# Second attention: maxima turned in 32x32 blocks and moved by DMAs instead of through TensorE

## What is computed

```python
# x (2, 1024, 128), 16 heads of 64
xn = rms_norm(x, gamma)
q, k, v = split(xn @ w_qkv)              # per head: 1024 x 64
sim = einsum('bhid,bhjd->bhij', q * 64 ** -0.5, k)
attn = softmax(sim, axis=-1)             # over the 1024 keys
out = einsum('bhij,bhjd->bhid', attn, v) @ w_out
```

## Time and profile before

| what | us |
|---|---|
| median of 3 runs | 1117.93 |
| lowest and highest run | 1117.87 and 1118.39 |
| span of the profiled execution, first to last instruction | 1115.6 |
| around that span, up to the median of the runs | 2.3 |
| granted TensorE clock, mean | 1.000 |

### The profile page before, as it was taken

One profiled execution on the slowest core, in us unless ns is written; L12 is line 12 of the kernel. 1 busy time (PEld: TensorE's weight loads), 2 busy tenths in 40 slices (PEclk: granted clock), 3 DMA queues, 4 the chain that ended last, 5 costly groups with the idle time before them and its releaser, 6 DMA issues.

```text
span 1115.6 us, 21181 instructions
## 1 busy us (share of the span) xinstructions
PE 1100.7 (99%) x8399; PEld 706.2 (63%) x8399; DVE 846.0 (76%) x1246; ACT 591.8 (53%) x939; POOL 795.7 (71%) x524
## 2 busy tenths in 40 slices
PE   9999999999999999999999999999999999999998
PEld 7899889777755555455455455455455555457886
DVE  4868897666686878878878888888888888896554
ACT  4534334566666555555555455555555555554443
POOL 5778888754367889888888888898889898950000
PEclk9999999999999999999999999999999999999999
DMA  7322223300000002000000000000000000000000
GB/s 251 127 77 80 95 77 115 94 24 1 1 1 1 1 1 105 1 1 1 1 1 1 1 1 1 1 1 1 1 1 1 1 1 1 1 1 10 9 1 19
DMA packets 25601, 30.97 MB, mean 28 GB/s; under 512 B 2064, under 2 KB 21904, under 8 KB 24224
## 3 DMA queue, kind: packets, MB, share of 16 engines
q1 hardware_dynamic: 25184, 29.62, 7.9%
q10 hardware_dynamic: 320, 0.01, 0.0%
HBM read 20.19 MB, written 9.44 MB: 27 GB/s over the span
## 4 chain that ended last, share of the span: by engine, by line
PE 88%; DVE 7%; issue 2%; ACT 2%; POOL 2%; DVEq 0%; POOLq 0%; ACTq 0%
PE o_ps L1713 19%; PE mx_ps L1667 7%; PE st_ps L1697 5%; PE st_ps L1691 5%; PE st_ps L1694 5%; PE ha_banks L647 5%; PE bank L2126 3%; PE bank L2127 3%; PE bank L2128 3%; PE mx_ps L1600 3%; PE pj_ps L1619 2%; PE pj_ps L1611 2%; PE ha_banks L698 2%; PE ha_banks L667 2%; PE ha_banks L709 2%
## 5 line engine op out<-in xcount | busy, mean ns | idle before, releaser
L2040 POOL TENSOR_TENSOR acc<-acc,prob 128x1024 f32<-128x1024 f32 x192 | 468.6, 2440 | 61.9 <-ACT prob L1861 51.7
L1861 ACT ACTIVATE prob<-st_ps 128x1024 f32<-128x1024 f32 x256 | 248.5, 1023 | 206.4 <-PE st_ps L1697 206.3
L1713 PE MATMUL o_ps<-prob,v_cur 128*64 128x512 f32 x1024 | 245.7, 599 | 0.0
L1932 DVE TENSOR_REDUCE mx_part<-mx_ps 128x1 f32<-128x512 f32 x258 | 164.9, 667 | 72.0 <-PE mx_ps L1667 72.0
L1713 PEld LDWEIGHTS o_ps<-prob,v_cur 128*64 128x64 f32 x1024 | 68.1, 136 | 96.2 <-issue 77.5
L1935 DVE TENSOR_REDUCE mx_part<-mx_ps 128x2 f32<-128x1024 f32 x78 | 93.7, 1201 | 44.1 <-PE mx_ps L1667 44.1
L1951 DVE RECIPROCAL rden<-rden 128x128 f32<-128x128 f32 x128 | 120.6, 942 | 0.0
L1667 PEld LDWEIGHTS mx_ps<-k_hi,q_hi 64*128 64x128 f32 x414 | 46.6, 183 | 107.0 <-issue 94.6
L1667 PE MATMUL mx_ps<-k_hi,q_hi 64*128 64x512 f32 x414 | 111.7, 457 | 1.5 <-DVE mx_part L1935 0.8
L1697 PE MATMUL st_ps<-q_hi,d_lo 64*128 64x512 f32 x512 | 100.8, 390 | 0.0
L2040 POOL TENSOR_TENSOR acc<-prob 128x1024 f32<-128x1024 f32 x32 | 76.1, 2378 | 26.2 <-PE pj_ps L1596 18.9
(11 more groups left out here) (419 smaller groups left out, 2349.3 us busy)
## 6 DMA issues: line engine op xcount, KB each, us to landing
v_rows<-ha_v SPq DMA_DIRECT2D x8, 1024.0 KB, 3.9
ha_vt<-v_rows SPq DMA_DIRECT2D x16, 512.0 KB, 4.0
h_w<-in_h SPq DMA_DIRECT2D x2, 1024.0 KB, 8.1
w_raw<-in_w SPq DMA_DIRECT2D x8, 192.0 KB, 3.2
head_wkv<-in_wkv SPq DMA_DIRECT2D x2, 512.0 KB, 6.0
m_w<-in_m SPq DMA_DIRECT2D x3, 256.0 KB, 3.1
out<-fin SPq DMA_DIRECT2D x3, 256.0 KB, 2.3
sel_raw<-in_sel SPq DMA_DIRECT2D x1, 576.0 KB, 11.5
```

The source lines that it names most:

```text
L1713: mm = pe.matmul(o_ps[rows(h), :], v_cur[:, m % 2, j, rows(h)], prob[:, (16 * m + slot) % RING, h, :], start=(j == 0), stop=(j == KT - 1), ...
L1861: act.activation(prob[:, n % RING, :, :], st_ps[:, slot % 2, :, :], ACT.Exp, scale=SCALE).then_inc(s_exp, 1)
L1932: dve.reduce_max(mx_part[:, h, i, keys:keys + 1], maxima_banks(q, n)[h], AX_X).then_inc(s_mxr, 1)
L2040: pool.tensor_tensor(total, old, new, ALU.add).then_inc(s_acc, 1)
```

## The change

The unit `("tr", half)` goes. `mx_row` becomes 128 x 32, of which eight columns are written. VectorE turns it in blocks of 32x32 into `mx_turned` right behind L1939, after waiting for its own result and for the DMAs that read the block before. SP gets a function `sync_max`, called for each half of each step: it waits for the turned block, and issues four DMAs, one for each block of 32 partitions. Each takes eight rows of 32 numbers and writes them into one row a head of `q_max` (partitions 0 and 64), all else in `q_max` stays zero from a fill at the start. The product with minus ones moves to the end of the slots 0, 1, 8 and 9, and waits for the DMAs in slots 0 and 8 alone. The pattern `diag` and its two DMAs go, and the load of the last network's weights is issued behind the DMAs of step 3.

```diff
-    mx_row = early.sb("mx_row", [P, 2, HD])
+    mx_row, mx_turned = early.sb("mx_row", [P, BLOCK], F32R), early.sb("mx_turned", [P, BLOCK])
...
-    BEFORE = (QK[0], QK[1], QK[2], ("tr", 1), QK[3], ("v", 0), ("v", 1), ("tr", 0))
+    BEFORE = (QK[0], QK[1], QK[2], None, QK[3], ("v", 0), ("v", 1), None)
...
-        sp.wait_ge(s_fill, 1)
-        sp.dma_start(diag[0:KT, :], a["diag"]).then_inc(s_wo, 16)
-        sp.dma_start(diag[HD:HD + KT, :], a["diag"]).then_inc(s_wo, 16)
...
+    def sync_max(sp, q, half):
+        sp.wait_ge(s_turned, 2 * q + half + 1)
+        if q:
+            sp.wait_ge(s_st, 16 * (q - 1) + KT * half + 2)
+        else:
+            sp.wait_ge(s_fill, 1)
+        heads = q_max[0:P:HD, half_of(half)].bitcast(F32).rearrange("h (i n) -> h i n", i=TT)
+        for block in range(TT):
+            of = slice(block * BLOCK, block * BLOCK + BLOCK)
+            sp.dma_start(heads[:, :, of], mx_turned[of.start:of.start + 2 * TT, :]).then_inc(s_max, 16)
...
-        elif u[0] == "tr":
-            pe.wait_ge(s_row, 2 * q + u[1] + 1)
-            for h in range(2):
-                mm = pe.matmul(to[rows(h), 0:P], mx_row[:, h, :], c.ident[:, :], start=True, stop=True,
-                               skip_group_check=True)
...
-        if fresh:
-            for h in range(2):
-                pe.matmul(st[:, h, :], minus[rows(h), :], q_max[rows(h), half_of(half)], start=True, stop=True)
...
+        if fresh:
+            if j == 0:
+                pe.wait_ge(s_max, 16 * TT * (2 * m + half + 1))
+            for h in range(2):
+                mm = pe.matmul(st[:, h, :], minus[rows(h), :], q_max[rows(h), half_of(half)], start=False, stop=True,
+                               skip_group_check=True)
...
-    def vector_spread_max(dve, q, u):
-
-        half = u[1]
-        dve.wait_ge(s_pj, count_of[q, u])
-        dve.tensor_tensor(q_max[:, half_of(half)].rearrange("p (i n) -> p i n", i=TT),
-                          unit_bank(q, u)[:, 0:P].unsqueeze(1).to_broadcast([P, TT, P]),
-                          diag[:, half_of(half)].rearrange("p (i n) -> p i n", i=TT), ALU.mult).then_inc(s_max, 1)
...
-            dve.reduce_max(mx_row[:, :, first:first + TT], mx_part[:, :, first:first + TT, :], AX_X)\
+            dve.reduce_max(mx_row[:, 0:2 * TT].rearrange("p (h i) -> p h i", h=2), mx_part[:, :, first:first + TT, :], AX_X)\
                .then_inc(s_row, 1)
+            turned = 2 * q + n // 8
+            dve.wait_ge(s_row, turned + 1)
+            if turned:
+
+                dve.wait_ge(s_max, 16 * TT * turned)
+            dve.transpose(mx_turned[:, :], mx_row[:, :].bitcast(F32)).then_inc(s_turned, 1)
...
-        if at_b and at_b[1][0] == "tr":
-            vector_spread_max(dve, *at_b)
...
-        pool.memset(diag[:, :], 0.0).then_inc(s_fill, 1)
+        pool.memset(q_max[:, :].bitcast(F32), 0.0).then_inc(s_fill, 1)
...
-                end.sync_raw(sp)
+                for m in range(STEPS):
+                    for half in range(HALVES):
+                        t2.sync_max(sp, m, half)
+                    if m == LOADED:
+                        end.sync_raw(sp)
```

More of the change, by code:

```diff
@@ L1366, in second_attention @@
     s = Const()
+    BLOCK = P // TT
     w_raw = early.sb("w_raw", [P, PAIRS, W_V])
     wo = early.sb("wo", [P, PAIRS, P])
-    diag = early.sb("diag_all", [P, LEN])
     q_max = early.sb("q_max", [P, LEN], F32R)
@@ L1401, in second_attention @@
     s_st, s_exp, s_acc, s_pv = (at.sem(n) for n in ("s_st", "s_exp", "s_acc", "s_pv"))
-    s_mx, s_mxr, s_row, s_max = (at.sem(n) for n in ("s_mx", "s_mxr", "s_row", "s_max"))
+    s_mx, s_mxr, s_row, s_turned, s_max = (at.sem(n) for n in ("s_mx", "s_mxr", "s_row", "s_turned1", "s_max"))
     s_v, s_den, s_osum, s_rcp, s_on, s_out = (
@@ L1422, in second_attention @@
     SLOT_CUT = 12
-    BEFORE = (QK[0], QK[1], QK[2], ("tr", 1), QK[3], ("v", 0), ("v", 1), ("tr", 0))
+    BEFORE = (QK[0], QK[1], QK[2], None, QK[3], ("v", 0), ("v", 1), None)
     AFTER = {1: ("den", 1), 3: ("out", 0), 5: ("den", 0), 7: ("out", 1)}
-    AHEAD = {**{u: 1 for u in QK}, ("v", 0): 1, ("v", 1): 1, ("tr", 0): 1, ("tr", 1): 0, ("den", 0): 0,
+    AHEAD = {**{u: 1 for u in QK}, ("v", 0): 1, ("v", 1): 1, ("den", 0): 0,
              ("den", 1): -1, ("out", 0): -1, ("out", 1): -1}
@@ L1440, in before @@
     def before(m, b):
+        if BEFORE[b] is None:
+            return None
         q = m + AHEAD[BEFORE[b]]
@@ L1503, in aside @@
         return three(q - AHEAD[u], b)
-    turns = [(0, QK[3]), (0, ("v", 0)), (0, ("v", 1)), (0, QK[2]), (0, ("tr", 0))]
+    turns = [(0, QK[3]), (0, ("v", 0)), (0, ("v", 1)), (0, QK[2])]
     turns += [u for m in range(STEPS + 1) for b in range(BATCHES)
@@ L1553, in unit_out @@
                 pe.wait_ge(s_d if t else s_lo, 2 * q + half + 1)
-        elif u[0] == "tr":
-            pe.wait_ge(s_max, 2 * q + u[1] + 1)
         elif u[0] == "v":
@@ L1578, in tensor_unit @@
             pe.wait_ge(e.s_su, e.ALL - 1)
-        elif (q, u) == (0, ("tr", 0)):
-            pe.wait_ge(s_row, 1)
         elif aside(q, u):
@@ L1615, in tensor_unit @@
             if q == 0 and half == 0:
-                pe.wait_ge(s_wo, 16 * (2 + PAIRS))
+                pe.wait_ge(s_wo, 16 * PAIRS)
             pe.wait_ge(s_on, 2 * q + half + 1)
@@ L1672, in tensor_scores @@
         half, j = slot // KT, slot % KT
-        if j == 0:
-            pe.wait_ge(s_max, 2 * m + half + 1)
         if m == 0 and slot == 0:
@@ L1685, in tensor_scores @@
         fresh = j < 2
-        if fresh:
-            for h in range(2):
-                pe.matmul(st[:, h, :], minus[rows(h), :], q_max[rows(h), half_of(half)], start=True, stop=True)
         upper = kh[:, tile(j)] if fresh else dh[:, tile(j - 2)]
         for h in range(2):
-            pe.matmul(st[:, h, :], upper[rows(h), :], qh[rows(h), half_of(half)], start=False, stop=False,
+            pe.matmul(st[:, h, :], upper[rows(h), :], qh[rows(h), half_of(half)], start=fresh, stop=False,
                       skip_group_check=True)
@@ L1696, in tensor_scores @@
         for h in range(2):
-            mm = pe.matmul(st[:, h, :], dl[rows(h), tile(j)], qh[rows(h), half_of(half)], start=False, stop=True,
+            mm = pe.matmul(st[:, h, :], dl[rows(h), tile(j)], qh[rows(h), half_of(half)], start=False, stop=not fresh,
                            skip_group_check=True)
+        if fresh:
[4 more added lines that the diff above has]
+                               skip_group_check=True)
         mm.then_inc(s_st, 1)
@@ L1744, in tensor_begin @@
         tensor_maxima(pe, 0, 8)
-        tensor_unit(pe, 0, ("tr", 0))
         tensor_maxima(pe, 0, 9)
@@ L1785, in unit_bank @@
             return st_ps[:, 0, QK.index(u), :]
-        if (q, u) == (0, ("tr", 0)):
-            return st_ps[:, 0, 0, :]
         return mx_ps[:, 1, :] if aside(q, u) else pj_ps[:, :]
@@ L1883, in vector_start @@
         dve.wait_ge(head.s_yc, head.TURNS)
-        dve.memset(mx_row[:, :, :], 0.0).then_inc(s_rowfill, 1)
+        dve.memset(mx_row[:, :].bitcast(F32), 0.0).then_inc(s_rowfill, 1)
         dve.memset(mx_part[:, :, :, :], 0.0).then_inc(s_rowfill, 1)
@@ L1967, in vector_begin @@
             vector_maxima(dve, 0, n)
-        dve.wait_ge(s_wo, 16 * (2 + PAIRS))
-        vector_spread_max(dve, 0, ("tr", 0))
         vector_maxima(dve, 0, 9)
@@ L2044, in second_attention @@
     s.tensor_begin, s.scalar_begin, s.vector_begin = tensor_begin, scalar_begin, vector_begin
+    s.sync_max = sync_max
     s.vector_start, s.gpsimd_start, s.gpsimd_begin = vector_start, gpsimd_start, gpsimd_begin
@@ L2396, in two_layers @@
         STARTED = 4
+        LOADED = 3
         SPLIT = 8
```

## The result

The changed kernel takes 1125.2 us (median of 4 runs, 1123.59 to 1125.79), the kernel before in the same session 1118.16 (1117.87 to 1118.42): the ratio is 1.0062, 95% interval 1.0047 to 1.0076. It is slower, by 7.0 us; the forecast was 1124.7. The profiled execution took 1125.26 with a span of 1123.0, so the 2.3 us around the span are unchanged, and the span grew by 7.4.

What follows compares the result with a forecast made beforehand. TensorE's and VectorE's chains reach the projection L1619 at the same moment, so TensorE wins nothing unless VectorE gets shorter. Terms +7.6 and -0.8 sum to +6.8 us: 1115.6 + 2.3 + 6.8 = 1124.7, range 1116 to 1136.

Steps and rivals of the forecast that it cites:

- What bounds it: At the projection L1619, TensorE's and VectorE's chains arrive together; TensorE wins nothing unless VectorE gets shorter.
- Step 1: Removed transposing matmuls on TensorE: 10.6 us in 28 steady batches, all falling into the projection's wait, put at 0.
- Step 2: Removed 32 products with the diagonal, 0.68 each, behind the last reduction: worth 0, only lengthening idle time.
- Step 3: Added VectorE transposition and wait before the reciprocal: 0.27 a batch, 28 times, 7.6 us (5.6 to 14.6).
- Step 4: Product with minus one moved from first to last in its slots, as many matmuls of the same shape: cost 0.
- Step 5: Four added SP DMAs per half: landed B+5.2 to B+5.7, needed at B+6.2 (B: batch start), cost 0.
- Step 6: Four other units: two in step 0 gain 0.8 us; one in step 15, 0; the start, 0 (-0.6 to +0.7).
- TensorE gets its time back: Rival: the bank does not hold the projection's load, batches end 0.38 earlier: -11.8 us, 1106.1; chance 0.13.
- The DMAs are late: Rival: slower issues land the DMAs 0.4 to 0.9 late on 28 halves, 11 to 25 us more: 1136 to 1150; chance 0.13.
- VectorE's addition hides: Rival: transposition slips under its neighbours and own wait is free: -0.8 to +2.0 us, about 1118.5; chance 0.10.

Runs made afterwards that it cites:

- experiment 2: Changed kernel with two unread matmuls of the removed shape put back in each of the 28 batches: 1123.71 us, ratio 1.0051.
- experiment 1: Kernel before, plus VectorE's wait for the row of maxima and a transposition into a tile nobody reads: 1124.69 us, ratio 1.0055.
- Experiment 3: Kernel before, with the reciprocal of the 28 batches moved behind the second reductions: 1118.01 us, ratio 0.9999.
- experiment 5: Changed kernel with eight unread matmuls ahead of TensorE's first wait for the DMAs: 1123.88 us, ratio 1.0048.
- experiment 4: Changed kernel with the reciprocal of the 28 batches moved behind the second reductions: 1109.80 us, ratio 0.9922.
- experiment 8: Changed kernel with eight DMAs of one head each for a half instead of four: 1206.88 us, ratio 1.0789.
- experiment 9: Kernel before, plus a VectorE transposition of a constant tile, without the wait for the row: 1119.96 us, ratio 1.0013.
- experiment 10: Changed kernel with the reciprocal moved, three unread matmuls before the first DMA wait, and ScalarE issuing two of the first four DMAs: 1107.86 us, ratio 0.9904.

## Why the prediction was right, and where it was not

The mechanism is the one forecast and its experiments hold it: the removed matmuls are worth nothing in the 28 batches (experiment 2), VectorE's addition sets the growth (experiment 1), and the number, 1124.7 for 1125.2, is nearer than its terms deserve; that nearness is luck. Term by term:

- *What bounds it.* Right, and closer than the text could know: both chains reach the projection at one moment. Experiment 3 shows TensorE's own chain alone at 2.27 after the row's reduction; VectorE's alone is worked out as 2.17 + 0.05 = 2.22.
- *Step 1, matmuls at 0.* Right: 10.6 us removed, 9.4 us of new idle time at L1618.
- *Step 2, products with the diagonal at 0.* Not tried by itself. In the trace after they are gone and VectorE idles there instead (1.60 ahead of the next batch's first maxima, 1.04 before).
- *Step 3, +7.6.* Right in kind, too high in size: 0.27 a batch was predicted, 0.19 measured and 0.02 in the batch behind it (5.9 us). The start after the row's reduction is 0.20, as predicted, the transposition holds up the next instruction by 0.14 instead of 0.16, the reciprocal is 0.03 shorter, and 0.05 of VectorE's time was hidden behind TensorE, for which the sum had no term. By the Trainium skill's rule on the emptied pipe (VectorE: DVE Perf Modes, "The DRAIN you can't avoid") the reciprocal would have begun at 722.30, after the 0.21 of the transposition; it began at 722.23. The prediction quoted that rule without the end of the same paragraph, "A next op that is not held starts earlier"; if the reciprocal is such an operation, the trace agrees, here and in the earlier trace rows.
- *Step 4, moved minus product at 0.* Right: 0.32 between second maxima and outputs, no pair longer.
- *Step 5, DMAs hidden.* Right in the 28 batches, with two errors that cancel. The issues are 0.54 apart, not 0.31 to 0.39, so the fourth starts at 722.33 + 3 x 0.54 = 723.95, B+3.93, not B+3.28. From there a transfer lands in 1.5, not 1.9 to 2.4: worked out from step 15, where TensorE waits for it, 3.17 after the block is turned. That is B+5.5, with L1697's load at B+6.13 a margin of 0.7. The fixed price of 2 us that the prediction took from the Trainium skill (DMA: Bandwidth & Descriptors, "Anatomy of one DMA") stands there for transfers that GpSimd issues; these are issued by SP.
- *Step 6.* The two units of step 0: −0.6 for −0.8. The start is the step that failed: 0 was predicted (−0.6 to +0.7) and it costs 2.7. The text gave the first half the margin of the steady batches, though there TensorE is through with slot 0's score products at 321.58, 2.5 us after the block is turned at 319.09, while the DMAs let it go 3.9 after; and it had no term for the clock. Some 1.2 are the wait's and 1.5 the clock's (experiments 2 and 5). Step 15 was predicted at 0 and came out 0.4 shorter: the batch that lost the unit gained 0.53, and the DMAs took back only 0.17 in the next:

```profile
972.15 0.21 DVE L1935 STREAM_TRANSPOSE mx_turned<-mx_row 128x32 f32<-128x32 f32 x1
972.39 2.11 SPq L1544 DMA_DIRECT2D q_max<-mx_turned  x4
975.53 0.18 PEld L1697 LDWEIGHTS st_ps<-q_max,minus 64*128 64x128 f32 x2 [0.33 <-DMA q_max<-mx_turned]
```

The sum's errors, −1.7 in step 3 and +2.5 in step 6 (+1.7 for −0.8), have nearly cancelled.

Of the rivals, "TensorE gets its time back" is the one that the experiments turned into a kernel: it does as soon as VectorE's chain becomes shorter (experiment 4). "The DMAs are late" came true at the start alone; in the steady batches it needed twice the issues, which experiment 8 made. "VectorE's addition hides" comes nearest in experiment 9, where the wait was taken out.

## What to carry to other kernels

When two engines reach the same bank at the same moment, cutting one is worth nothing and lengthening the other costs nearly in full (here 0.19 of 0.22): look for the wait that names both, and shorten both together. The order of an engine's list is the cheapest means: a reciprocal that nobody waits for, moved behind two reductions that TensorE waits for, turned a change of +0.6% into −0.8%, while the same move by itself gave nothing. For small DMAs count the issues one by one, and look at the first use in a loop separately, where nothing hides them.

## What the runs showed of the hardware that was not expected

- One wait of 1.85 us in front of a weight load (1.41 of TensorE) at the start was followed by 3.4 us at a granted clock of 0.50. It is not certain to follow: the changed kernel ran 1123.59 in a run at clock 1.000, experiment 2 kept its clock in the profiled execution behind the same wait, and in experiment 8 only nine of 32 waits of 1.7 to 4.1 us were followed by it. Its price is 1.4 us over two batches (7.25 + 5.38 against 5.72 + 5.52).
- The issue of a small DMA between tiles on the core takes 0.50 (four a half) or 0.57 (eight a half, one head each), against the 0.27 and 0.35 in the earlier trace rows; the first ones of the changed kernel took 0.66 and 0.55, and the first one on ScalarE in experiment 10 took 1.36. Why was not tried.
- A transposition of 128x32 takes 0.21 and holds up the next instruction by 0.14. The wait for VectorE's own result just before it costs nearly as much, 0.12.
- The reciprocal of 128x128 took 0.91 behind a transposition and 0.94 behind a reduction, in all batches; the reason stays open.
